# Cross-attention and a ternary feed-forward block: the last result in one VectorE instruction, the down projection moved, the transposed x in two places

## The reference

```python
def xattn(h, ctx):                       # 16 heads of 128
    q = rmsnorm((h @ Wq).reshape(B, Sq, H, D), gq)
    k = rmsnorm((ctx @ Wk).reshape(B, Skv, H, D), gk)
    v = (ctx @ Wv).reshape(B, Skv, H, D)
    attn = softmax(einsum('bqhd,bkhd->bhqk', q, k) / sqrt(D))
    return einsum('bhqk,bkhd->bqhd', attn, v).reshape(B, Sq, H * D) @ Wo

def h_bitlinear(x, w):                   # Hadamard rotation, 8-bit activations, ternary weights
    return einsum('bsh,oh->bso', act_quant(fwht(x)), weight_quant(w))

def ffn(h):
    return h_bitlinear(silu(h_bitlinear(h, w_gate)) * h_bitlinear(h, w_up), w_down)

x = x + xattn(layernorm(x), ctx)
x = x + ffn(layernorm(x))
```

## Time and profile before

| what | value |
|---|---|
| median of three runs | 1473.45 us (1469.47, 1473.45, 1475.27) |
| the profiled execution | 1468.72 us |
| its span, from the first to the last instruction or transfer | 1466.8 us |
| TensorE busy | 1427.9 us (97%) |
| VectorE, ScalarE, GpSimd busy | 65%, 65%, 36% |
| end of the last query matmul | 184 us into the span |
| DMA, mean | 113 GB/s |

### The profile page before, as it was taken

One profiled execution on the slowest core, in us unless ns is written; L12 is line 12 of the kernel. 1 busy time (PEld: TensorE's weight loads), 2 busy tenths in 40 slices (PEclk: granted clock), 3 DMA queues, 4 the chain that ended last, 5 costly groups with the idle time before them and its releaser, 6 DMA issues. The chain is left out here.

```text
span 1466.8 us, 30515 instructions
## 1 busy us (share of the span) xinstructions
PE 1427.9 (97%) x8997; PEld 1225.7 (84%) x8997; DVE 954.2 (65%) x2464; ACT 947.1 (65%) x2069; POOL 524.0 (36%) x323
## 2 busy tenths in 40 slices
PE   8999989999999999999999999999899999999998
PEld 8888868999999989989999999998767677767765
DVE  5312056677777777777777777766467677767774
ACT  4556568878888878888788888887433334333432
POOL 0033324433322233323332333334244555555533
PEclk9999999999999999999999999999999999999999
DMA  7767723343444434343344434335533222322211
GB/s 238 215 180 195 206 78 85 103 110 106 116 125 117 120 105 116 112 130 110 106 122 124 115 110 115 105 83 140 158 118 88 71 57 64 95 69 57 64 32 40
DMA packets 187783, 165.07 MB, mean 113 GB/s; under 512 B 111040, under 2 KB 162256, under 8 KB 185872
## 3 DMA queue, kind: packets, MB, share of 16 engines
q1 hardware_dynamic: 180752, 151.21, 37.7%
q10 hardware_dynamic: 6912, 12.59, 2.7%
HBM read 123.44 MB, written 33.14 MB: 107 GB/s over the span
## 5 line engine op out<-in xcount | busy, mean ns | idle before, releaser
L707 POOL TENSOR_TENSOR rk_sp<-ms_sp,neg_half 76x10 f32<-76x10 f32 (+1 forms) x128 | 244.2, 1925 | 594.0 <-DMA ms_sp<-ms 594.0
L1030 DVE CUSTOM_DVE_ANT_0 sc<-psS,rk 100x361 f32<-100x361 f32 x256 | 136.3, 532 | 106.6 <-PE psS L765 82.9
L882 ACT ACTIVATE pr<-ex,ri 100x361 f32<-100x361 f32 x256 | 152.8, 597 | 81.5 <-DVE ri L1019 81.3
L875 ACT ACTIVATE ex<-sc,nb,rq 100x361 f32<-100x361 f32 x256 | 175.2, 684 | 8.5 <-DVE nb L1037 8.4
L741 PE MATMUL psK<-cT_hi,wk_hi 128*128 128x362 f32 x512 | 169.9, 332 | 1.7 <-DVE k_lo L1000 1.7
L863 ACT ACTIVATE k_hi<-psK 128x362 fp32r<-128x362 f32 x256 | 120.8, 472 | 76.1 <-PE psK L741 75.0
L741 PE MATMUL psK<-cT_lo,wk_hi 128*128 128x362 f32 x512 | 167.7, 328 | 0.0
L741 PE MATMUL psK<-cT_hi,wk_lo 128*128 128x362 f32 x512 | 167.7, 328 | 0.0
L1000 DVE TENSOR_TENSOR k_lo<-psK,k_hi 128x362 fp32r<-128x362 f32 x256 | 134.4, 525 | 6.7 <-ACT sq L869 5.4
L790 PE MATMUL psZ<-pT_hi,cK_hi 120*128 120x400 f32 (+1 forms) x384 | 132.8, 346 | 0.0
L790 PE MATMUL psZ<-pT_hi,cK_lo 120*128 120x400 f32 (+1 forms) x384 | 132.3, 344 | 0.0
(11 more groups left out here) (177 smaller groups left out, 3582.9 us busy)
## 6 DMA issues: line engine op xcount, KB each, us to landing
rk<-rk_dram SPq DMA_DIRECT2D x64, 564.1 KB
o_in<-o_dram SPq DMA_DIRECT2D x13, 1024.0 KB, 6.0
q_dram<-q_out SPq DMA_DIRECT2D x64, 200.0 KB, 4.4
q_in<-q_dram SPq DMA_DIRECT2D x64, 200.0 KB, 4.9
o_dram<-o SPq DMA_DIRECT2D x64, 200.0 KB, 5.3
stage<-in_w_ff SPq DMA_DIRECT2D x12, 1024.0 KB, 6.7
w_in<-in_w_ff ACTq DMA_DIRECT2D x48, 256.0 KB, 3.1
cT_in<-in_ctxT SPq DMA_DIRECT2D x16, 361.0 KB, 5.0
```

Source lines behind the costliest of these rows:

```text
L707: nc.gpsimd.tensor_tensor(rk_sp[:, cols], ms_sp[:, cols], neg_half[0:HG * SKR, :].to_broadcast([HG * SKR, n]), op=ALU.pow).then_inc(g_rk, 1)
L875: nc.scalar.activation(ex[:, h % 2, :], sc[:, h % 2, :], ACT.Exp, bias=nb[:, h % 2:h % 2 + 1], scale=rq[:, j % 2, h:h + 1], accum_out=rs[: ...
L882: nc.scalar.activation(pr[:, h, :], ex[:, h % 2, :], ACT.Copy, scale=ri[:, h % 2:h % 2 + 1]).then_inc(a_pr, 1)
L1030: nc.vector.tensor_tensor_reduce(out=sc[:, h % 2, :], in0=psS[0:SQ, 0:SK], in1=rk[:, j % 2, h, :], scale=1.0, scalar=-3.0e38, op0=ALU.mult ...
```

## The change

Four things are changed. In the queries, `xT_hi` and `xT_lo` have two places, used in turn by the groups; chunks 0 and 1 are split in front of head 12 and chunks 2 and 3 in front of head 15, and the waits on `p_read` give way to one on the end of the group before the last. The loops over groups 1 and 2 are written out on all five engines. In the feed-forward end, step 11 has the down projection of tile 11 and 13 filler matmuls where it had 27 filler matmuls, so that the down projection is ahead of the transposes. For the last tile, VectorE makes y with one instruction (scale and add the residual, straight from PSUM), in place of ScalarE's scaling and GpSimd's addition, and the residuals are not shifted any more.

```diff
-        xT_hi, xT_lo = sb("xT_hi", [P, DC, GT], F32R), sb("xT_lo", [P, DC, GT], F32R)
+        xT_hi, xT_lo = (sb(n, [P, 2, DC, GT], F32R) for n in ("xT_hi", "xT_lo"))
...
+        XT_AT = {12: (0, 1), 15: (2, 3)}
...
-                        if h == H - 1 and c < DC - 1:
-                            last.then_inc(p_read, 1)
...
-            with pe.Fori(1, G - 1) as g:
+            for g in range(1, G - 1):
                 group(g, False, False)
...
-            def high_xT(g):
+            def high_xT(g, c):
                 act.wait_ge(p_xT, g * GB + GB)
-                for c in range(DC):
-                    if c < DC - 1:
-                        if due((g - 1) * (DC - 1) + c + 1):
-                            act.wait_ge(p_read, (g - 1) * (DC - 1) + c + 1)
-                    else:
-                        if due(g * H):
-                            act.wait_ge(p_q, g * H)
-                    nc.scalar.activation(xT_hi[:, c, :], psX[c][:, 0:GT], ACT.Copy).then_inc(a_xhi, 1)
+                if due((g - 1) * H):
+                    act.wait_ge(p_q, (g - 1) * H)
+                nc.scalar.activation(xT_hi[:, g % 2, c, :], psX[c][:, 0:GT], ACT.Copy).then_inc(a_xhi, 1)
...
-                    if h == H - 1 and not last:
-                        high_xT(g + 1)
+                    for c in XT_AT.get(h, ()):
+                        if not last:
+                            high_xT(g + 1, c)
...
-                sp.wait_ge(g_y, t + 1 if isinstance(t, int) else sp.snap(t + 1))
+                if last_tile(t):
+                    sp.wait_ge(v_y, 1)
+                else:
+                    sp.wait_ge(g_y, t + 1 if isinstance(t, int) else sp.snap(t + 1))
...
-                if real(i):
-                    result(i)
-                move_residuals(i)
+                if not last_tile(i):
+                    if real(i):
+                        result(i)
+                    move_residuals(i)
...
-                if isinstance(i, int) and i == TILES - 2:
-                    busy(psA, 27)
+                late = isinstance(i, int) and i == TILES - 2
+                if late:
+                    down(i, 0, front)
+                    down(i, 1, front)
+                    busy(psA, 13)
                 if real(i + 1):
                     hidden_T(i + 1, 0)
                     hidden_T(i + 1, 1)
...
-                if real(i):
+                if real(i) and not late:
                     down(i, 0, front)
                     down(i, 1, front)
...
+            def last_result(t):
+
+                dve.wait_ge(p_down, t + 1)
+                dve.wait_ge(d_out, t * 16)
+                dve.wait_ge(g_old, (t + 2) * 2)
+                dve.wait_ge(v_scale[1], 5 * t + 5)
+                nc.vector.scalar_tensor_tensor(y[:], psF[:], ald[:], x1[:, 0, :], ALU.mult, ALU.add).then_inc(v_y, 1)
```

More of the change, by code:

```diff
@@ L159, in queries @@
         used = [s("used1_0"), s("used1_1")]
-        p_xT, p_read, a_xhi, v_xlo = s("p1_xT"), s("p1_read"), s("a1_xhi"), s("v1_xlo")
+        p_xT, a_xhi, v_xlo = s("p1_xT"), s("a1_xhi"), s("v1_xlo")
         p_q, a_q = s("p1_q"), s("a1_q")
@@ L229, in _ @@
             group(0, False)
-            with sp.Fori(1, G - 1) as g:
+            for g in range(1, G - 1):
                 group(g, False)
@@ L268, in _ @@
             group(0, True, False)
-            with pool.Fori(1, G - 1) as g:
+            for g in range(1, G - 1):
                 group(g, False, False)
@@ L328, in group @@
                         for w, m in ((wq_hi, xT_hi), (wq_hi, xT_lo), (wq_lo, xT_hi)):
-                            last = nc.tensor.matmul(psQ[h % 2][:, 0:GT], w[:, c, h * D:(h + 1) * D], m[:, c, :],
+                            last = nc.tensor.matmul(psQ[h % 2][:, 0:GT], w[:, c, h * D:(h + 1) * D], m[:, g % 2, c, :],
                                                     start=(n == 0), stop=(n == 3 * DC - 1))
                             n += 1
-                        if h == H - 1 and c < DC - 1:
-                            last.then_inc(p_read, 1)
                     last.then_inc(p_q, 1)
@@ L346, in _ @@
             group(0, True, False)
-            with pe.Fori(1, G - 1) as g:
+            for g in range(1, G - 1):
                 group(g, False, False)
             group(G - 1, False, True)
-            busy(psX[0], wq_hi[:, 0, 0:P], xT_hi[:, 0, :], 4)
+            busy(psX[0], wq_hi[:, 0, 0:P], xT_hi[:, 0, 0, :], 4)
             squares(G - 1, NG - 1)
-            busy(psX[0], wq_hi[:, 0, 0:P], xT_hi[:, 0, :], 6)
+            busy(psX[0], wq_hi[:, 0, 0:P], xT_hi[:, 0, 0, :], 6)
             factors(G - 1)
@@ L408, in _ @@
             split_first(0)
-            high_xT(0)
+            for c in range(DC):
+                high_xT(0, c)
             split_first(1)
             group(0, True, False)
-            with act.Fori(1, G - 1) as g:
+            for g in range(1, G - 1):
                 group(g, False, False)
@@ L464, in mean_squares, with low_xT @@
                 nc.vector.tensor_scalar(ms[:], psS[:, 0:GT], D * EPS, None, ALU.add).then_inc(v_ms, 1)
[L466 to L471, removed]
+            def low_xT(g, c):
+                dve.wait_ge(a_xhi, g * DC + c + 1)
+                nc.vector.tensor_tensor(xT_lo[:, g % 2, c, :], psX[c][:, 0:GT], xT_hi[:, g % 2, c, :].bitcast(F32),
+                                        ALU.subtract).then_inc(v_xlo, 1)
             def group(g, first, last):
                 for h in range(H):
-                    if h == H - 1 and not last:
-                        low_xT(g + 1)
+                    for c in XT_AT.get(h, ()):
+                        if not last:
+                            low_xT(g + 1, c)
                     if first and h in SPLIT_AT:
@@ L496, in _ @@
             split_first(0)
-            low_xT(0)
+            for c in range(DC):
+                low_xT(0, c)
             split_first(1)
             group(0, True, False)
-            with dve.Fori(1, G - 1) as g:
+            for g in range(1, G - 1):
                 group(g, False, False)
@@ L1150, in real, with last_tile @@
             return not isinstance(t, int) or 0 <= t < TILES
+        def last_tile(t):
+            return isinstance(t, int) and t == TILES - 1
         def pipeline(eng, step, reach):
@@ L1508, in step @@
                     high_o(i + 3)
-                if real(i):
+                if real(i) and not last_tile(i):
                     scale_down(i)
@@ L1680, in rotate_across @@
                 nc.vector.tensor_tensor(half_rot[:, 0:2, :], hid[:, 0:2, :], hid[:, 2:4, :], ALU.add).then_inc(v_r2, 1)
+            def last_result(t):
[4 more added lines that the diff above has]
+                nc.vector.scalar_tensor_tensor(y[:], psF[:], ald[:], x1[:, 0, :], ALU.mult, ALU.add).then_inc(v_y, 1)
             def step(i):
+                if last_tile(i):
+                    last_result(i)
                 if real(i + 1):
```

2 lines of the change are left out of this document (1 added, 1 removed).

## The result

The changed kernel took 1462.68 us (median of 6 runs, 1460.85 to 1464.11), the kernel before beside it 1473.2 us (6 runs, 1469.47 to 1475.27): ratio 0.9932, 95% interval [0.9917, 0.9947], so 8 to 12 us faster. Forecast were 1467.5 us, a range from 1463.3 to 1472.8, and 4.9 us of gain. Two more comparisons later gave 0.9947 [0.9931, 0.9962] and 0.9944 [0.9932, 0.9957]; over the three it is about 0.994, 8 to 9 us.

A forecast was written before the change was run, and what follows sets the result against it. TensorE, busy for 97% of the span, was taken as the bound. Terms 2.12 + 0.96 + 1.1 + 0.7 = 4.9 us gave 1468.55 from the median, 1466.6 from the middle of four executions; forecast between them 1467.5, range 1463.3 to 1472.8.

The forecast's parts named there:

- Down projection ahead of the transposes: Feed-forward end: tile 12's Hadamard product starts at 1443.99 instead of 1446.11; gain 2.12 us, bounds 1.9 and 2.2.
- Last result on VectorE: Very end: last product to store's issue takes 1.14 us instead of 2.10; gain 0.96 us, bounds 0.6 and 1.3.
- Two places for the transposed x: Second and third query group boundaries: pitches of 0.91 and 0.86 us fall to 0.33; gain 1.1 us, at most 1.5.
- Groups written out: Queries: SyncE issues each weight load 0.26 us earlier, shortening TensorE's waits; gain 0.7 us, between 0 and 1.2.
- two query terms: Queries: the gains forecast for two places for the transposed x, 1.1 us, and for groups written out, 0.7 us.
- Rival 2: Queries: all stalls on weight loads in groups 1 and 2 go, upper bounds hold elsewhere; 6.2 us gain, 1465.3; 10%.
- Rival 1: Queries: loads from DRAM set the pace, so only the end's 3.1 us count; 1468.4 us; 20%.
- rival 4: Feed-forward end: transposes come late or the Hadamard product waits for something else; 2.8 us remain, 1468.7; 5%.
- Rival 3: Feed-forward end: the gap before the Hadamard product halves TensorE's clock; 10.0 us slower, 1481.5; 3%.

The follow-up runs named there:

- down_early: The kernel before with only tile 11's down projection moved ahead of the transposes and 13 fillers for 27: ratio 0.9983, 2.5 us faster.
- last_only: The kernel before with only the last result made in one VectorE instruction: ratio 0.9993 [0.998, 1.0005], 1.0 us.
- before_loads: The kernel before with the third and fourth load of feed-forward weights of each group issued one head earlier: ratio 0.9963, median 1463.1 us.
- before_again: The kernel before, unchanged, run once more: ratio 0.9995, median of ten 1469.2 us; its profiled execution took 1472.81 us.
- unroll_only: The kernel before with query groups 1 and 2 written out on all five engines, nothing else: ratio 0.9985, 2.2 us faster.
- q_at15: The kernel before with the queries' part of the change, but all four chunks split in front of head 15: ratio 0.9980, 2.9 us faster.
- ctx_later: The kernel before, loops kept, with the four transfers of attention's first context issued behind the store of head 1 of the last group: ratio 1.0001.
- q_only: The kernel before with only the queries' part of the change: ratio 0.9974 [0.9960, 0.9989], 3.8 us faster.
- loads_ff: The kernel before with the feed-forward half of the change and the third and fourth weight loads one head earlier: ratio 0.9945, median 1460.55 us.
- after_loads: The changed kernel with the third and fourth weight loads one head earlier: ratio 0.9942 to the kernel before, median 1460.33 us.

## Why the prediction was right or wrong

**Down projection ahead of the transposes, 2.12 us: right.** 2.3 us in down_early's trace, 2.5 in its times. The Hadamard product waits 0.98 us for its operand, as worked out. The transposes start within 0.06 us of the end of VectorE's last rotation, as they did.

**Last result on VectorE, 0.96 us: right in the mechanism, 0.3 low.** 1.28 us in the trace of last_only. The term that was mis-sized is the lag from TensorE to VectorE, taken as 0.35 from an addition with several waits behind the one that ends last; it was 0.04. So the 0.38 of the earlier trace rows is not a price of waits that are already met. A nearer row was in the trace of before, the instruction that the new one replaces. ScalarE waits for the same last product, with two more waits behind it, and starts 0.04 us after its end (1462.27):

```profile
1462.31 0.69 ACT L1487 ACTIVATE y<-psF,ald 128x512 f32<-128x512 f32 x1 [6.77 <-PE psF L1384]
```

The instruction's 0.75 us were right.

**Two places for the transposed x, 1.1 us: the wait goes as forecast, its cause was read one link short.** The pitch over the boundaries falls to 0.19, not 0.33, which is worth 1.4 us. But the step said that the low part is late because ScalarE splits only in front of head 15. before_loads splits there too and loses nothing beyond 0.33 - 0.19 = 0.14 us. It is late because ScalarE comes from a late fourth load. The prediction had that load in its next paragraph, as the cause of head 15's stall alone.

**Groups written out, 0.7 us: this step failed.** It took 0.5 us off the wait at head 15 of the second group, 0.2 off smaller waits, and nothing off the last group, as its code is unchanged. The traces show it the other way round. The stall at head 15 of the second group is 0.8 us in the mean of the five traces of before's queries and 0.65 in the four of the changed ones, so it hardly moves. The last group is where the time goes: its stalls fall from 2.4 us to 1.2 in the mean, and its length from 42.2 (the half clock of before_again taken off) to 41.1. All five are longer than all four, and than unroll_only and q_at15. By the times unroll_only gains 2.2 us; its interval, 0.6 to 3.8, would still hold 0.7, so it is the place more than the size that these runs refute. Why the last group gets shorter stays open: the first load goes out 0.8 to 1.6 us earlier there, but ctx_later, which brings that about in another way, showed no gain in its times.

The two query terms together were 1.8 us, upper bound 2.7. Measured: 3.8 us in the times of q_only, and 189.9 less 186.1 (mean of 185.43, 185.62, 184.86 and 188.60) = 3.8 us in the traces, 3.2 with the half clock taken off.

**The sum.** 3.8 + 3.6 = 7.4 us by the traces (6.8 with the half clock taken off), about 8.5 by the three comparisons, and 4.9 forecast. Of the difference 2.0 us are the query terms, 0.5 the feed-forward's, and about 1 us has no place. The first comparison's 10.5 us between the medians is at the upper end of what the later ones allow; how much of that difference is chance and how much the chip can't be said. The prediction noted that its execution was 4.7 us faster than the median of three runs, and took its 4.9 us from 1472.4, close to that median. The later runs say that the execution was the better base: their medians lie 0.1 us below to 0.9 us above it.

**Rivals.** Rival 2 (the written-out code gains more) was the nearest, given 10%; its 6.2 us were still low, and its reason, that the stalls on the loads in groups 1 and 2 all go, did not come true, as 0.53 us is left at head 15. Rival 1 (the queries give it back) is refuted by q_only, rival 4 by the trace. Rival 3, the clock, did not happen: an idle time of 0.98 us ahead of the Hadamard product leaves the granted clock full. Two sides of it were read too lightly. The earlier trace rows cannot show a full clock, as a spell of 3 us at half clock leaves a slice of 36.7 us above 90%; the sum over before's trace does, with 1.00 up to 1464.7. And the clock does fall in this kernel: behind the first 16 us it does so six times in the seventeen traces, each after a wait of 1.8 to 2.6 us. Waits of 1.85 us (last_only, 36.2) and 1.97 us (ctx_later, 208.5) left it full, so the length of one wait does not decide it. The warning of the Trainium skill ("TensorE: Matmul & The Clock Gate", "Why this matters for your kernels") does not bite on a gap of this length in this trace.

## What to carry to other kernels

Size a gain by the stalls of more than one trace. Two executions of the same kernel differed by 4 us here, and a median of three runs lay 4 to 5 us above those of the hundred that followed. Before such a difference is put down to waits, sum the granted clock over short stretches: most of it was three spells of half clock, which the page's tenths hide. Follow a late engine back to the first thing that made it late: two stalls a head apart, one by an output, one by a split, were one late load, and moving two loads by one head was worth at least as much as a second buffer and written-out loops. Where a stage waits for transfers, a change can also move the waits of a part whose code it leaves alone. Filler work in front of a wait is the place to look for real work that lies behind it.

## What was not expected of the hardware

A VectorE instruction with four waits, the first of which ends last, started 0.04 us after TensorE's modelled end in all seven traces that have it, while an addition in the steady part started 0.38 us behind the earlier trace rows. ScalarE's scaling of y, the same instruction in every tile, starts 0.20 us behind in the ten tiles of the loop and 0.04 in the three that are written out, in the trace of before. What makes these lags differ wasn't found.

TensorE's clock fell to half for some 3 us after waits of 1.79, 1.88 and 1.94 us in one execution of the kernel before, and not once before its last product in another with waits of 1.57 and 1.71 us. Six runs of before_loads have a mean clock of 0.9997 and six of loads_ff 0.9998, where before has 0.9984 to 0.9986. So part of what the earlier loads gain may be clock; after_loads, at 0.9987, does not show it.

And three context transfers that take 1.29 us to issue in the kernels with all loops written out took 1.87 to 2.7 us where the other engines had loops, with SyncE's own code written out or not, and 2.1 us in ctx_later, where they are issued one head into the last group. The cause of that wasn't found.
